# Layer 0 of a graph network on one core: keys of the destination one-hots spread by a transfer instead of TensorE

## What is computed

```
h   = relu(layernorm(x))
Q, K, V = h @ Wq, h @ Wk, h @ Wv
q_dst = Q[dst] + rel_q[type];  k_src = K[src] + rel_k[type] + edge_attr @ Wt + bt
v_src = V[src] + rel_v[type]
decay = exp(decay_scale * tanh(relu([w, type'] @ Wd1 + bd1) @ Wd2 + bd2))
dist  = |m[src] - m[dst]|                      # m: h mapped into a ball
logits = alpha * sum_head(q_dst * k_src) / 4 * decay - (1 - alpha) * beta * dist * decay
attn  = softmax of the logits over the edges of one dst
x     = x + ffn(layernorm(h + segment_sum(v_src * attn, dst) @ Wo + bo))
```

## Time and profile before

| | us |
|---|---|
| median of 3 runs | 4676.12 (4672.93 to 4678.23) |
| span of the profiled execution | 4669.4 |
| layer 0's main loop, first to last L1210 | 204.8 to 1793.1 |

### The profile page before, as it was taken

How to read it: one execution, slowest core, us unless ns; L and a number is a source line. 1 busy time by engine, 2 the same in 40 slices (tenths; PEclk the granted TensorE clock), 3 DMA queues, 4 the chain that set the end, 5 groups by cost and what they waited for, 6 DMA issues and landing times.

```text
span 4669.4 us, 87216 instructions
## 1 busy us (share of the span) xinstructions
PE 3495.5 (75%) x31645; PEld 2819.8 (60%) x31645; DVE 3310.1 (71%) x6623; ACT 2081.9 (45%) x6143; POOL 1899.3 (41%) x2178
## 2 busy tenths in 40 slices
PE   1488888887887886326666468885789999969996
PEld 1255555454554553216666467774489999859995
DVE  5467666665666665459998687886766666679997
ACT  2344444444545443237887356673022222224443
POOL 0355576665666665100000130000045555538884
PEclk7788898888999997668777688997899999979998
DMA  4655555565555553010000221112344444313332
GB/s 105 191 154 157 157 167 153 160 152 149 164 165 156 163 163 100 13 38 10 12 11 10 58 83 53 44 44 87 113 125 127 121 128 127 104 54 129 127 129 69
DMA packets 368023, 498.51 MB, mean 107 GB/s; under 512 B 76530, under 2 KB 307636, under 8 KB 367453
## 3 DMA queue, kind: packets, MB, share of 16 engines
q1 hardware_dynamic: 313437, 328.51, 23.2%
q0 software_dynamic: 54144, 164.25, 12.6%
HBM read 381.76 MB, written 110.84 MB: 105 GB/s over the span
## 4 chain that ended last, share of the span: by engine, by line
PE 35%; DVE 23%; issue 11%; POOL 11%; ACT 11%; another core or an unknown queue 4%; DMA 3%; SPq 2%; ACTq 0%; DVEq 0%; POOLq 0%
POOL arena_a L1172 9%; PE psum L3699 4%; PE psum L3715 3%; PE psum L3650 3%; PE psum L3648 3%; PE psum L3002 3%; ACT arena_c L2965 2%; PE psum L3615 2%; POOL arena_c L1210 2%; DVE arena_a L3195 2%; PE psum L3674 2%; PE psum L3287 2%; PE psum L3697 2%; ACT arena_a L1366 2%
## 5 line engine op out<-in xcount | busy, mean ns | idle before, releaser
L1172 POOL DMA_INDIRECT arena_a<-src_table,src_tix x808 | 820.8, 1016 | 433.0 <-issue 385.9
L3419 POOL TENSOR_SCALAR node_hot<-arena_c 128x128 fp32r<-128x128 f32 x575 | 369.9, 654 | 901.6 <-DVE arena_c L3307 569.6
L3437 DVE SCALAR_TENSOR_TENSOR msg_parts<-psum,msg_parts 128x512 fp32r<-128x512 f32 (+2 forms) x644 | 425.6, 661 | 260.6 <-ACT msg_parts L3586 228.4
L3137 POOL TENSOR_SCALAR node_hot_dst<-arena_c 128x128 fp32r<-128x128 f32 x587 | 384.5, 671 | 121.9 <-DVE arena_c L3541 67.9
L3002 PE MATMUL psum<-arena_a,arena_c 128*128 128x150 f32 x1800 | 289.6, 331 | 173.3 <-ACT arena_c L2968 173.3
L3586 ACT ACTIVATE msg_parts<-psum 128x512 fp32r<-128x512 f32 (+2 forms) x325 | 186.5, 574 | 520.3 <-PE psum L3650 520.3
L3648 PE MATMUL psum<-arena_c,arena_a 128*128 128x128 bf16 x3675 | 406.4, 220 | 0.0
L3650 PE MATMUL psum<-arena_c,arena_a 128*128 128x128 bf16 x3675 | 406.4, 220 | 0.0
L3002 PEld LDWEIGHTS psum<-arena_a,arena_c 128*128 128x128 f32 x1800 | 284.0, 225 | 176.5 <-ACT arena_c L2968 176.5
L1352 ACT ACTIVATE arena_c<-psum 128x272 f32<-128x272 f32 x404 | 160.9, 398 | 467.5 <-remote 396.6
L1366 ACT ACTIVATE arena_a<-arena_a 128x128 f32<-128x128 f32 x808 | 238.6, 300 | 291.2 <-issue 226.7
(11 more groups left out here) (583 smaller groups left out, 10197.9 us busy)
## 6 DMA issues: line engine op xcount, KB each, us to landing
y_rows<-arena_c SPq DMA_DIRECT2D x101, 576.0 KB
arena_a<-bucket_rows SPq DMA_DIRECT2D x150, 384.0 KB
arena_a<-bucket_rows SPq DMA_DIRECT2D x50, 448.0 KB
arena_a<-bucket_lists SPq DMA_DIRECT2D x25, 896.0 KB
pair_counts<-arena_c SPq DMA_DIRECT2D x25, 800.0 KB
arena_a<-bucket_lists SPq DMA_DIRECT2D x25, 704.0 KB
arena_a<-src_table,src_tix POOLq DMA_INDIRECT x808
arena_c<-edge_attr SPq DMA_DIRECT2D x101, 128.0 KB
```

The costliest lines, as they stand in the source:

```text
L1172: e.indirect_dma_start(out_, None, table, bass.IndirectOffsetOnAxis(ap=idx, axis=0)).then_inc(sem, 16)
L3137: return e.tensor_scalar(node_hot3[at % RING_H][:, i, :], iota_row, dst_lo[:, b, t:t + 1], None, ALU.is_equal)
L3419: return e.tensor_scalar(node_hot[at % RING_M][:, i, :], iota_row, src_lo[:, b, 2 * k + j:2 * k + j + 1], None, ALU.is_equal)
L3437: e.scalar_tensor_tensor(out=to[:, 1, 0:nt, :], in0=bank[at % 4][:, 0:nt * P].rearrange("p (t f) -> p t f", f=P), scalar=0.0, in1=to[:, 0, ...
```

## The change

The keys reach ACT by a transfer. Ahead of the loop the kernel computes for every edge the key less its block's first node, at most N - WIN, in bf16: PE multiplies a 0/1 matrix `first_tile` with the tiles' first keys, so that every tile gets the first key of its block, and DVE subtracts it (`near_h`). SP stores that list to `near_keys`. In the loop SP loads for block n+2 the 1024 near keys broadcast to 126 partitions and the 1024 types broadcast to the last 2 (`near_row`, 2 KB a partition), where it had loaded `hlt`.

ACT makes the differences of a block in one instruction over 1024 columns, from SBUF, with the bias column `minus_place`, the same for all blocks. Differences, picks and window parts of block n+1 stand at the head of ACT's turn n. `pick_w` and `win_parts` have three buffers instead of two (`RING_P`), so that this may run ahead of PE's products. PE's two `pe_w_pick` a turn are gone, and so are the waits for bank 3 that went with them. The waits of the other two users of the keys' semaphores are renumbered; their code runs in a branch that isn't taken.

```diff
@@ ahead of the loop
+            e.wait_ge(g.lists_set, 7)
+            e.dma_start(near_keys.rearrange("(c p f) -> p c f", p=P, f=P), near_h).then_inc(g.d_lists, 16)
...
-            e.wait_ge(g.d_lists, 288)
+            e.wait_ge(g.d_lists, 304)
...
+            e.wait_ge(g.type_pe, 3)
+            own.step(e.tensor_scalar(block_first, bank[5][:, 0:TC], float(N - WIN), None, ALU.min))
+            e.tensor_tensor(near_h, keys_f[:, DST], bc(block_first, 2, P), ALU.subtract).then_inc(g.lists_set, 1)
...
+            e.wait_ge(g.tr_dve, 3)
+            e.matmul(bank[5][:, 0:TC], first_tile, keys_f[:, DST, :, 0], start=True, stop=True).then_inc(g.type_pe, 1)
@@ SP, in the loop
+        def sp_load_near_keys(e, k):
+            s = k % 2
+            if k >= 2:
+                e.wait_ge(g.pick_ready, k - 1)
+            e.dma_start(near_row[s][0:WIN, :], row_bc(near_keys[key_slice(k)], WIN)).then_inc(g.d_hlt[s], 16)
+            e.dma_start(near_row[s][WIN:P, :], row_bc(dst_hl[2, key_slice(k)], NET)).then_inc(g.d_hlt[s], 16)
...
                         sp_window(e, j, dst_win, 2 * D, 0)
-                        sp_load_window_keys(e, j, 0)
+                        sp_load_near_keys(e, j)
@@ ACT
-        def act_w_differences(e, k, hf):
-
-            s = k % 2
-            if k >= 2:
-                e.wait_ge(g.q_pe, 2 * (k - 1))
-            e.wait_ge(g.picks_pe, 2 * k + hf + 1)
-            e.activation(pick_w[s][:, 4 * hf:4 * hf + 4, :], bank[3][:, :].rearrange("p (t f) -> p t f", t=4), ACT.Abs,
-                         bias=minus_node[:, k:k + 1]).then_inc(g.pick_ready, 1)
+        def act_w_differences(e, k):
+
+            s = k % RING_P
+            if k >= RING_P:
+                e.wait_ge(g.q_pe, 2 * (k - RING_P + 1))
+            e.wait_ge(g.d_hlt[k % 2], 32 * turns(k, 2))
+            e.activation(pick_w[s][:, :, :], near_row[k % 2].rearrange("p (t f) -> p t f", t=TPB), ACT.Abs,
+                         bias=minus_place).then_inc(g.pick_ready, 1)
...
+                if ahead:
+                    act_w_differences(e, n + 1)
+                    act_w_picks(e, n + 1)
+                    act_w_high(e, n + 1)
                 if b1:
                     act_w_squares(e, i1, 0)
...
-                if ahead:
-                    act_w_differences(e, n + 1, 0)
                 if b1:
                     act_w_squares(e, i1, 1)
...
-                if ahead:
-                    act_w_differences(e, n + 1, 1)
...
-                if ahead:
-                    act_w_high(e, n + 1)
-                    act_w_picks(e, n + 1)
@@ PE
-                if n + 1 < NBLK:
-                    pe_w_pick(e, n + 1, 0)
...
-                if n + 1 < NBLK:
-                    pe_w_pick(e, n + 1, 1)
...
                 if b0:
-                    if n + 1 < NBLK:
-                        e.wait_ge(g.pick_ready, 2 * (n + 2))
                     e.wait_ge(g.hid_act, i0 + 1)
```

More of the change, by code:

```diff
@@ L426, in program @@
         run_rows = dram("run_rows", [2, TC * P, P])
+        near_keys = dram("near_keys", [TC * P * P], BF16)
         t16_row = dram("t16_row", [1, TC * P * P])
@@ L479, in program @@
         hlt = [arena_b[0:3, o_ + s * TPB * P // 2:o_ + (s + 1) * TPB * P // 2].bitcast(BF16) for s in range(2)]
+        near_row = [arena_b[:, o_ + s * TPB * P // 2:o_ + (s + 1) * TPB * P // 2].bitcast(BF16) for s in range(2)]
         GD = [arena_b[:, s * TPB * 2 * D:(s + 1) * TPB * 2 * D].rearrange("p (t w) -> p t w", t=TPB) for s in range(RING_D)]
@@ L545, in part_buffers @@
             return [nc.alloc_sbuf_tensor_at(f"{name}{i}", shape, F32R, offset=base + 4 * (at + i * size)) for i in range(n)]
[L548 to L551 removed]
+        RING_P = 3
+        rows4_at = 2 * TPB * (P + D + H + WMAX + P // 2)
+        pick_w = (part_buffers("pick_w", base_b, RING_W * 2 * D, 2, [P, TPB, P])
+                  + part_buffers("pick_w_last", base_c, rows4_at, 1, [P, TPB, P]))
+        win_parts = (part_buffers("win_parts", base_w, 0, 2, [P, 2, 2 * D])
+                     + part_buffers("win_parts_last", base_c, rows4_at + TPB * P, 1, [P, 2, 2 * D]))
+        minus_place = weights0[:, 8 * D:8 * D + 1]
         half_row = weights0[:, 8 * D + NBLK:8 * D + NBLK + TPB]
@@ L559, in program @@
         type_h = arena_b[:, 6 * TC * P:6 * TC * P + TC * P // 2].bitcast(BF16).rearrange("p (c f) -> p c f", c=TC)
+        near_h = arena_b[:, 6 * TC * P + TC * P // 2:7 * TC * P].bitcast(BF16).rearrange("p (c f) -> p c f", c=TC)
+        first_tile, block_first = same[0][:, 0, :], small[0][:, 0, 0:TC]
         src_c, dst_c, src_t, dst_t = (tmp_f[:, i] for i in (4, 5, 0, 1))
@@ L1864, in dve_l0_windows @@
             o_ = (TPB - 1) * H
-            e.tensor_scalar(minus_node, win_node[:, :], -1.0, None, ALU.mult)
+            own.step(e.tensor_scalar(minus_place, is_node[:, :], -float(WIN), float(WIN), ALU.mult, ALU.add))
+            e.tensor_tensor(minus_place, minus_place, iota_col, ALU.subtract)
             e.memset(half_row, 0.5)
@@ L2392, in pe_pick @@
             s = k % 2
-            e.wait_ge(g.d_hlt[s], lane_base(s, 2, layers, 16) + 16 * turns(k, 2))
+            e.wait_ge(g.d_hlt[s], lane_base(s, 2, layers, 32) + 16 * turns(k, 2))
             if after_same:
                 e.wait_ge(g.same_ready, after_same)
-            if 2 * (layers * NBLK + k) + hf:
-                e.wait_ge(g.pick_ready, 2 * (layers * NBLK + k) + hf)
+            e.wait_ge(g.pick_ready, NBLK + 2 * k + hf)
             e.matmul(bank[2][:, :], win_w[:, :], hlt[s][:, hf * 512:(hf + 1) * 512], start=True, stop=True).then_inc(g.picks_pe, 1)
-        def pe_w_pick(e, k, hf):
-            s = k % 2
-            e.wait_ge(g.d_hlt[s], 16 * turns(k, 2))
-            if hf:
-                e.wait_ge(g.pick_ready, 2 * k + 1)
-            elif k:
-                e.wait_ge(g.hid_act, k)
-            e.matmul(bank[3][:, :], win_w[:, :], hlt[s][:, hf * 512:(hf + 1) * 512], start=True, stop=True).then_inc(g.picks_pe, 1)
         def pe_keep_busy(e, k):
```

40 lines of the change are left out of this document (19 added, 21 removed).

## The result

The changed kernel takes 4482.99 us (4473.01 to 4485.94), the kernel before on the same chip 4677.17 us (4672.93 to 4684.44): a ratio of 0.9584, 95% interval 0.9568 to 0.9600. The forecast was 4636 us, the range began at 4565. The change is faster, and by 4.2% where 0.9% was forecast.

The account below looks back on a forecast made before the run. Layer 0's loop was taken as bound by PE signals held until the last gather lands, delaying ACT's squares. Span 4669.4 - 43.4 + 3 = 4629.0 us, with the median 6.7 us above span: 4636 us, range 4565 to 4709.

Parts of the forecast that it names:

- The bound: Layer 0's main loop: POOL's distances wait for ACT's squares, ACT for PE's pair 1 signal; about 16.04 us a turn.
- Part 3: PE loses two L2408 a turn (0.74 us) and waits on ACT's L1383; worth nothing, clock about the same.
- The release: Moment in a usual loop turn when PE's held signals arrive, once the last gather has landed: +13.7 us, expected unchanged.
- Part 1: ACT's turn: differences become one activation at the head, so L1383 leaves the stretch before the squares: -43.4 us, bounds 21 to 50.
- The clock: PE's granted clock in the loop, 0.99 and 0.79 of full speed in alternating turns; about the same expected after the change.
- Part 2: Head of ACT's turn: moved work adds 0.40 us against 1.72 us of idle cover, so nothing counted.
- part 4: Loop's 256 KB near_row load, 0.91 us of all 16 DMA engines, fits free time: 0 taken, bound 0.91 us a turn.
- Part 5: Once only, ahead of the loop: near_keys store +1.5 us and first load at the loop's start +1.5, together +3 us.
- Signals are held less often: Rival, chance 0.12: PE gives fewer signals and starts earlier; 25 more turns of 13.04 us save 57 us: 4579 us.

Follow-up runs that it names:

- e15: Changed kernel with ACT's old order, two PE products and PE's two old waits for ACT back, ACT not waiting for PE: 4577.03 us, ratio 0.9961.
- e17: Changed kernel with two unread PE products a turn and their signals put back, without waits for ACT's differences: 4517.00 us, ratio 0.9646 (before 4685.73).
- e8: Changed kernel with ACT's old order (differences as two halves at old places, picks and high part at turn's end): 4452.06 us, ratio 0.9713.
- e7: The changed kernel itself timed again, on one chip with e8 and e9: 4446.25 us, ratio 0.9712 (before 4586.31).
- e14: Kernel before without PE's three unread filler products a turn: ratio 1.0033 (before 4366.27 us).
- e5: The changed kernel itself timed again beside the kernel before (4585.15 us): 4450.85 us, ratio 0.9704.
- e6: Changed kernel with near keys loaded only for the first two blocks, so later picks are wrong: 4452.32 us, ratio 0.9694.
- study 1: Four variants (ACT's old order, PE products put back, squares first in either kernel) where before took 4367.79 us: ratios 1.0029, 1.0027, 0.9997, 1.0025.
- e18: Kernel before with each gather of layer 0's loop replaced by a plain load of the same size: 4293.14 us, ratio 0.9824 (before 4369.33).
- e13: Changed kernel with ACT's old order, two PE products back and ACT waiting for their signals, PE not waiting for ACT's differences: ratio 1.0033 (before 4366.27 us).
- e9: Kernel before with the second half's squares ahead of ACT's copy of pair 1: 4552.79 us, ratio 0.9930 (before 4586.31).
- e1: Changed kernel with ACT's old order, the same kernel as e8, where before took 4367.79 us: ratio 1.0029.

## Why the prediction was wrong

**The bound was read rightly.** ACT's copy of pair 1 waits for the signal of a product whose record had ended long before, and squares and distances follow. The updates themselves show it (1334.33 to 1340.24).

**Part 3 failed**: "PE isn't what ends the turn, the release is, so its 0.74 us and its waits are worth nothing on their own". The release was taken as a fixed point at +13.7, set by the last gather. It isn't fixed: in the changed kernel it was at +10.9 in the turn shown, before the last gather was issued. Nor was it one moment before: DVE's L1853 went on at 1338.13 and ACT's copy at 1340.27. PE's waits for ACT were what closed a loop: signals are held, so ACT copies and makes differences late, so L2498 and PE's whole next turn start late. These are medians over the turns of held traces, us from POOL's mark (the nearest one for PE's next turn, the one before for the rest):

| | PE's next turn begins | pair 1's products end | ACT's copy of pair 1 starts | turns under 13.3 us |
|---|---|---|---|---|
| before | +2.85 | +9.35 | +13.70 | 7 |
| e15 | +2.73 | +9.35 | +12.85 | 8 |
| e17 | +1.25 | +8.99 | +11.44 | 33 |
| changed kernel | +0.63 | +8.97 | +11.28 | 40 |
| e8 | +0.62 | +8.37 | +10.08 | 45 |

The last link, from an earlier PE to an earlier signal, is argued and not shown: PE begins 2.2 us earlier in the changed kernel, but pair 1's products end only 0.4 us earlier, and the copy starts 2.4 us earlier.

What PE's waits are worth is measured. e15 puts only the products and PE's two waits back and is at 0.9961, where e8, the same kernel without them, is at 0.9713: 2.5 points, some 114 us, of which e17 leaves the products about 0.6. Of the waits I weighed L2408's 128.1 us and passed over L2498's 116.6, which held PE at +1.05 and let its next turn begin at +2.95. That the waits, not ACT's wait for PE, carry it is shown by e15, which has no wait of ACT. How far the products count is shown only across two studies, and with ACT's new order; ACT's old order with the products and without the waits has no held run.

**Part 1 was mis-sized.** 43.4 us for L1383's place measured 6 us (e8 beside e7), inside their spread. It was worked out on turns that ACT ends; POOL waits for the squares in 47 turns of the changed kernel, where it did in 89 of the same 101. Even the whole reordering, squares first, gave the kernel before only 33 us.

**The clock** (part 3): about the same was forecast; over 1200 to 1600 us the granted clock rose from 0.91 to 0.98 of the full 2.4 GHz (before, then changed).

```profile
1200.00:1600.00 400.00, 332.92 (x1492) 206.82 (x1492) 251.69 (x488) 200.57 (x769) 246.95 (x231) 0.91 0.56 162
```

```profile
1200.00:1600.00 400.00, 359.23 (x1708) 222.67 (x1708) 293.65 (x582) 240.72 (x893) 295.41 (x275) 0.98 0.74 213
```

PE has less work a turn but more of it a microsecond (359.23 beside 332.92 busy us). So the rule of the Trainium skill (TensorE: Matmul & The Clock Gate, What's actually happening) that activity releases the throttle speaks for this change, not against it, as I had set it out; by that rule the trace agrees, and e14 agrees from the other side.

**Part 2 and part 4 held.** The new instruction takes 1.13 us (1.09 forecast). In the loop it waits for the load twice, 20.9 us in all, both times behind a DMA that occupied SP's queue for 27.83 us:

```profile
ACT pick_w L1402 <- DMA arena_b<-dst_hl: 20.9, 2, 14.3
```

```profile
967.10 27.83 SPq L964 DMA_DIRECT2D npos<-end_pos  x1
```

The kernel before has the same DMA (28.19 us), and the two turns around it take 52.1 us in the changed kernel and 51.7 in the other, so the new wait costs next to nothing even there. The transfer doesn't lengthen the held loop by anything near the 0.91 us a turn of the bound: e5 and e6 are within 1.5 us.

**Part 5**: the loop starts 4.9 us later (+3 forecast), in study 1 3.3 to 5.4.

**The rivals.** "Signals are held less often" was the right one, with a chance of 0.12. I gave it 25 turns and 57 us. There were 33 more turns under 13.3 us, and the loop gave 187 us: some 124 from these turns, which fell from a mean of 16.26 to 12.50 us, and 63 from the 60 others, whose mean fell to 15.21. The rival's name fits the signal that ACT's squares stood behind: the copy of pair 1 starts over 1 us after its products' end in 64 of 101 turns, before in 93. It doesn't fit PE's signals as a whole: 42% of them come in time, before 38%. I argued against it with turns in which PE had been equally early by its own start and were held; but I compared turns within a kernel in which PE's waits were all in place.

**What the prediction could not know** is that the same kernel takes 4368 us elsewhere. There the change looks like a loss of 0.3%: the seven runs of kernels with the transfer gave 1.0025 to 1.0038. The changed kernel itself was not timed there.

**Open.** What holds PE's signals, and what decides the condition; whether gathers are needed for it (e18 met no hold); e13 and e14 in the held condition. Transfers stay under suspicion: over the waits of more than 2 us before ACT's copies, between 205 and 1500 us, the median of DMA packets under way fell from 14 half a microsecond before the wait ended to 0 half a microsecond after it in the kernel before (80 waits), and from 13 to 4 in the changed one (91). But a POOL that waits issues no gathers either, so this shows no cause. Why an earlier PE gets its signals through is seen, not explained.

## What to carry to other kernels

An engine that doesn't end a turn can still close a loop: before pricing its waits at nothing, follow them into the next turn, and ask whether what they wait for is itself late. A moment that recurs at the same place in every turn may be set by the loop itself, and not be a fixed event. And where a profile shows remote waits, compare the producer's record with the signal's arrival, and time both kernels in more than one place: this change is worth 3 to 4% where signals are late, and its near variants cost 0.3% where they are not.

## What was new about the hardware

- PE's semaphore updates can come up to 6 us after the product's record ends and then 0.04 us apart; in the traces of the free studies at least 98% come within 0.05 us of it. The time of the kernel before differs by 7% between the two conditions (4366 and 4686 us).
- Where the updates are late, 19 to 25% of them are missing from the record; in the free traces it is 2% at most.
- A mean gather issue of POOL took between 999 (e9) and 1033 ns (e1) in these kernels; no pair of runs shows what sets it.
- With three filler products of 512 columns a turn the mean granted clock is 0.89, without them 0.862, and the kernel without them is 0.3% slower in the free condition (e14).
